# A vision block on one Trainium2 core: the attention operand stack stored as 128 rows, the position tables written in one transfer, and an earlier start

## What is computed

```
h = einsum('bhid,oi,od->bho', x, weighted_sum, weight)        # 32 x 512 x 256
q, k, v = heads of layernorm(h) @ W + b                        # 16 heads of 16
rel = log_bucket(i - j)                                        # 128 buckets, 64 either way
c2p = take(q . pos_k, rel + 64);  p2c = take(k . pos_q, -rel + 64), swapped
probs = softmax((q . k + c2p + p2c) / scale);  h += (probs . v) @ Wo + bo
h += mixture of 8 experts, 512 tokens each, of layernorm(h)
```

## Time and profile before

| | us |
|---|---|
| median of 3 runs | 5152.89 |
| the runs | 5137.70, 5157.19, 5152.89 |
| the profiled execution, its own time | 5136.03 |
| its span in the profile | 5134.3 |
| project with set-up | 0 to 981 |
| attend | 981 to about 4315 |
| output, choice, experts | from there to 5134 |

### The profile page before, as it was taken

One profiled execution on the slowest core, in us unless ns is written; L12 is line 12 of the kernel. 1 busy time (PEld: TensorE's weight loads), 2 busy tenths in 40 slices (PEclk: granted clock), 3 DMA queues, 4 the chain that ended last, 5 costly groups with the idle time before them and its releaser, 6 DMA issues. The chain is left out here.

```text
span 5134.3 us, 108898 instructions
## 1 busy us (share of the span) xinstructions
PE 4635.4 (90%) x30952; PEld 3294.1 (64%) x30952; DVE 3490.0 (68%) x9093; ACT 2706.1 (53%) x5074; POOL 1858.2 (36%) x4429
## 2 busy tenths in 40 slices
PE   6999999589999999999999999999999997894699
PEld 4666666366666666666666666666666665673556
DVE  2333333378888878888878887888888886776511
ACT  1222222266666666667666666666666664441111
POOL 1222222144444444444444444444444443330032
PEclk9999999799999999999999999999999999886599
DMA  4767676699999999999999999999999997663033
GB/s 135 229 222 233 222 236 222 198 339 354 352 337 351 350 332 346 348 334 354 348 339 348 346 346 333 346 341 332 349 350 352 349 349 231 211 216 103 2 92 81
DMA packets 663054, 1444.73 MB, mean 281 GB/s; under 512 B 47635, under 2 KB 289731, under 8 KB 662339
## 3 DMA queue, kind: packets, MB, share of 16 engines
q1 hardware_dynamic: 656326, 1429.44, 82.3%
q0 software_dynamic: 6144, 8.52, 0.9%
HBM read 722.89 MB, written 714.89 MB: 280 GB/s over the span
## 5 line engine op out<-in xcount | busy, mean ns | idle before, releaser
L1010 DVE CUSTOM_DVE_ANT_1 a_scored<-a_ps_m_s,a_bias 128x512 f32<-128x512 f32 x2048 | 1398.6, 683 | 565.4 <-PE a_ps_m_s L878 538.9
L947 ACT ACTIVATE a_probsT<-a_ps_m_t 128x512 f32<-128x512 f32 x2048 | 1226.0, 605 | 931.6 <-PE a_ps_m_t L887 930.0
L887 PE MATMUL a_ps_m_t<-a_ident,a_scored 128*128 128x128 f32 x8192 | 1261.9, 277 | 0.5 <-ACT a_probsT L947 0.5
L941 ACT ACTIVATE a_skew_in<-a_ps_m_tab 128x512 f32<-128x512 f32 x2048 | 1124.0, 613 | 192.6 <-DMA d_skew<-a_skew_in 130.8
L887 PEld LDWEIGHTS a_ps_m_t<-a_ident,a_scored 128*128 128x128 f32 x8192 | 937.1, 141 | 437.4 <-DVE a_scored L1017 358.9
L1017 DVE TENSOR_SCALAR a_scored<-a_scored,a_top_of 128x512 f32<-128x512 f32 x2048 | 1044.5, 530 | 0.0
L827 POOL TENSOR_SCALAR_AFFINE_SELECT a_bias<-a_bias 128x128 f32<-128x128 f32 (+2 forms) x2560 | 984.0, 411 | 71.8 <-POOL a_bias L827 63.1
L818 POOL COPY a_bias<-a_high 128x128 f32<-128x128 f32 (+1 forms) x1024 | 357.9, 378 | 1741.4 <-DMA a_bias<-d_skew 1740.3
L878 PE MATMUL a_ps_m_s<-a_ident,a_bias 128*128 128x128 f32 x5120 | 901.3, 273 | 0.0
L859 PE MATMUL a_ps_m_tab<-a_tabs,a_stack 96*128 96x256 bf16 (+1 forms) x4096 | 714.3, 276 | 183.7 <-ACT a_skew_in L941 111.9
L878 PEld LDWEIGHTS a_ps_m_s<-a_ident,a_bias 128*128 128x128 f32 x5120 | 682.7, 142 | 108.3 <-issue 2.1
(11 more groups left out here) (193 smaller groups left out, 3937.9 us busy)
## 6 DMA issues: line engine op xcount, KB each, us to landing
d_skew<-a_skew_in SPq DMA_DIRECT2D x1024, 480.0 KB, 7.7
a_bias<-d_skew SPq DMA_DIRECT2D x512, 896.0 KB, 8.8
a_stack<-d_stack SPq DMA_DIRECT2D x256, 384.0 KB
p_xt<-in_xT SPq DMA_DIRECT2D x32, 2048.0 KB, 9.2
d_ctx<-a_ctx_sb SPq DMA_DIRECT2D x128, 256.0 KB, 7.8
d_stack<-p_part_q SPq DMA_DIRECT2D x64, 384.0 KB, 2.8
d_stack<-p_part_k SPq DMA_DIRECT2D x64, 384.0 KB, 3.4
d_v<-p_v_sb SPq DMA_DIRECT2D x32, 544.0 KB, 3.0
```

What stands on the lines that cost most here:

```text
L887: mm = pe.transpose(m_t[:, k % 2, t * P:(t + 1) * P], scored[:, hh % SCORED, t, k * P:(k + 1) * P], ident[:])
L941: nc.scalar.activation(skew_in[:, u, w, 2 * half:2 * half + 2], m_tab[:, w], ACT.Identity).then_inc(tab_kept, 1)
L947: nc.scalar.activation(turned_at(hh // GH, hh % GH, k), m_t[:, k % 2], ACT.Exp, scale=SCALE).then_inc(turned, 1)
L1010: nc.vector.tensor_tensor_reduce(split(scored[:, hh % SCORED, t]), split(m_s[:, t % 2]), extra, 1.0, -3.0e38, ALU.add, ALU.max, top_of[:, ...
```

## The change

- `d_stack` has eight lanes instead of six: lane 7 is zeros. Lane 6 holds the nine terms' rows: in the key half the key terms, in the query half ones for the queries to which they apply (all, those of tile 2 and up, those of tile 3), and three rows of ones in the key half for the tables' constant part. `d_kterm` is gone. A new constant `extra` (128 rows, two lanes) is written into lanes 6 and 7 for every batch by two transfers of 128 rows of 4 KB; the key terms follow in six small transfers over it instead of two, once the `extra` of that batch has landed.
- `key_terms` writes four groups of 32 output rows with 128 columns each (16 matmul instructions instead of 4), so that the result is 128 x 128 and not 32 x 512.
- The stack is loaded whole: one transfer of 128 rows of 2 KB a head. No ones are set in attend.
- `scores` is one matmul of 128 rows and 512 columns for each t; `tables` use 128 rows; `tabs` is 128 rows with cleared rows where there is no operand (cleared by VectorE and GpSimd, whole).
- Table writes are one transfer over 128 partitions with all 1024 columns.
- Set-up: the products `mix` come first, `x` of batch 0 is loaded from ScalarE's queue, and the four mixing tiles of batch 0 stand between TensorE's steps of the set-up.
- Start of attend: the first stack pair is loaded before `tabs`, half of `tabs` is loaded from ScalarE's queue, and the first table writes and reads stand between the loads of stacks 3 to 6.

```diff
-        d_stack = dram("d_stack", (B, NH, HD, SLOTS, SW), BF16)
+        d_stack = dram("d_stack", (B, NH, HD, LANES, SW), BF16)
...
+            @block.scalar
+            def _(act):
+                act.dma_start(xt[:, 0], xT[0].rearrange("d (c p) s -> p (d c) s", p=P)).then_inc(x_in[0], 16)
+                act.dma_start(extra_f[:], io["extra"]).then_inc(extra_in, 16)
+                act.wait_ge(extra_in, 16)
+                nc.scalar.activation(extra[:, 0], extra_f[:], ACT.Identity).then_inc(extra_set, 1)
...
             def _(pe):
+                pe.wait_ge(t_dve, 1)
+                pe.wait_ge(x_in[0], 16)
+                mix_tile(pe, 0, 0)
                 pe.wait_ge(t_dve, 6)
...
+                mix_tile(pe, 0, 1)
                 pe.wait_ge(t_dve, 7)
...
+                mix_tile(pe, 0, 2)
                 pe.wait_ge(t_dve, 8)
...
+                mix_tile(pe, 0, 3)
                 pe.wait_ge(t_dve, 19)
...
                     n = 2 * i + u
+                    for c in range(HC):
+                        sp.dma_start(d_stack[n, c * NH // HC:(c + 1) * NH // HC].rearrange("h d j x -> (h d) j x")[:, SLOTS:],
+                                     extra[:]).then_inc(extra_out, 16)
                     if not last:
...
-                    to = d_kterm[n].rearrange("t h x -> h t x")
-                    sp.dma_start(to[:, 0:3], part_t[0:NH]).then_inc(t_out, 16)
-                    sp.dma_start(to[:, 3:], part_t[NH:]).then_inc(t_out, 16)
+                    settled(sp, extra_out, 16 * HC * (n + 1), passed)
+                    to = d_stack[n, :, :, SLOTS]
+                    for j in range(QT):
+                        for side in range(2 if j < 2 else 1):
+                            at, d = (2 * j + side) * NH, 3 * side * (j + 1)
+                            sp.dma_start(to[:, d:d + 3, S + j * P:S + (j + 1) * P], part_t[at:at + NH]
+                                         ).then_inc(t_out, 16)
...
-                    mm = pe.matmul(m_t[:], kterm_w[:, c], full_k[:, c], start=(c == 0), stop=(c == HC - 1))
+                    for j in range(QT):
+                        mm = pe.matmul(m_t[j * 2 * NH:(j + 1) * 2 * NH], kterm_w[:, c], full_k[:, c, j * P:(j + 1) * P],
+                                       start=(c == 0), stop=(c == HC - 1), skip_group_check=True)
...
-                sp.dma_start(stack[0:ST, u], d_stack[b, g * SH:(g + 1) * SH].rearrange("h d j x -> (d j) h x")
-                             ).then_inc(stack_in[u], 16)
-                sp.dma_start(stack[ST:ST + TERMS, u, :, S:], d_kterm[b, :, g * SH:(g + 1) * SH]
+                sp.dma_start(stack[:, u], d_stack[b, g * SH:(g + 1) * SH].rearrange("h d j x -> (d j) h x")
                              ).then_inc(stack_in[u], 16)
...
-                half, used = P // 2, QT * TW - P // 2
-                for p0, x0 in ((0, half), (half, 0)):
-                    sp.dma_start(bass.AP(scratch, slot * P * PITCH + p0 * (PITCH + 1) + x0,
-                                         [[PITCH + 1, half], [ROW, 2], [1, used]]),
-                                 skew_in[p0:p0 + half, u].rearrange("p w t x -> p w (t x)")[:, :, x0:x0 + used]
-                                 ).then_inc(skew_out[u], 16)
+                sp.dma_start(bass.AP(scratch, slot * P * PITCH, [[PITCH + 1, P], [ROW, 2], [1, QT * TW]]),
+                             skew_in[:, u].rearrange("p w t x -> p w (t x)")).then_inc(skew_out[u], 16)
...
-            sp.wait_ge(zeroed_p, 4)
-            for g in range(SR - 1):
+            sp.dma_start(past[:], io["past"]).then_inc(past_in, 16)
+            load_stack(0, 0)
+            load_tabs(sp, 0)
+            sp.wait_ge(tabs_clear[1], 1)
+            sp.dma_start(tabs[PLAIN_AT:PLAIN_AT + LANES * (PLAIN - 1) + 1:LANES, 1], d_plain).then_inc(const_in, 16)
+            sp.dma_start(ident[:], io["ident"]).then_inc(const_in, 16)
+            for g in range(1, SR - 1):
+                if g == 3:
+                    for m in range(2):
+                        write_tables(m, m, m)
+                    read_tables(0, 0, 0)
                 load_stack(0, g)
+                if g >= 3 and g - 1 < LEAD:
+                    write_tables(g - 1, g - 1, g - 1)
+                    if g - 2 < NEXT:
+                        read_tables(g - 2, 0, g - 2)
...
-                far = max(0, t - 1) * P
-                if far:
-                    pe.matmul(bank[:, 0:far], row[:, t * P:(t + 1) * P], row[:, S:S + far], start=True, stop=False,
-                              skip_group_check=True)
-                pe.matmul(bank[:, far:], row[0:ST + 3, t * P:(t + 1) * P], row[0:ST + 3, S + far:], start=not far,
-                          stop=False, skip_group_check=True)
+                pe.matmul(bank[:], row[:, t * P:(t + 1) * P], row[:, S:], start=True, stop=False, skip_group_check=True)
...
-            nc.vector.memset(tabs[ST:, 1], 0.0).then_inc(zeroed_p, 1)
+            nc.vector.memset(tabs[:, 0], 0.0).then_inc(tabs_clear[0], 1)
             nc.vector.memset(m_ctx[:], 0.0).then_inc(zeroed_p, 1)
-            nc.vector.memset(stack[ST:, 0], 1.0).then_inc(zeroed_p, 1)
-            nc.vector.memset(stack[ST:, 1:], 1.0).then_inc(zeroed_p, 1)
```

More of the change, by code:

```diff
@@ L166, in project, with mix_tile @@
     kterm_w = sb("kterm_w", [P, HC, 2 * NH])
-    kterm_bias = sb("kterm_bias", [2 * NH, 1])
+    kterm_bias = sb("kterm_bias", [P, 1])
     minus_half = sb("minus_half", [P, QT])
     xt = sb("xt", [P, 2, ND * HC, S])
+    extra = sb("extra", [P, LANES - SLOTS, SW], BF16)
+    extra_set, extra_zero = sem("p_extra_set"), sem("p_extra_zero")
     xT = io["xT"]
     x_in = [sem(f"p_x_in{u}") for u in range(2)]
+    h_done = sem("p_h_done")
+    m_h = ps("m_h", [P, QT, H])
+    def mix_tile(pe, u, t):
+        for k in range(ND * HC):
+            mm = pe.matmul(m_h[:, t], xt[:, u, k, t * P:(t + 1) * P], mix[:, k],
+                           start=(k == 0), stop=(k == ND * HC - 1))
+        if t % 2:
+            mm.then_inc(h_done, 1)
     with ExitStack() as tctx:
@@ L254, in step @@
                         dve.wait_ge(t_dve, done[0])
+                dve.wait_ge(t_mix, 32)
+                for d in range(ND):
+                    for c in range(HC):
+                        nc.vector.tensor_tensor(mix[:, d * HC + c], ws[:, c], wd[:, d], ALU.mult)
                 dve.wait_ge(t_in, 16 * len(loads))
@@ L402, in mixing @@
                     after(pe, h_kept, 2 * (n - 1) + t // 2 + 1 if not isinstance(n, int) or n else 0)
-                for k in range(ND * HC):
-                    mm = pe.matmul(m_h[:, t], xt[:, u, k, t * P:(t + 1) * P], mix[:, k],
-                                   start=(k == 0), stop=(k == ND * HC - 1))
-                if t % 2:
-                    mm.then_inc(h_done, 1)
+                mix_tile(pe, u, t)
             def turn(n):
@@ L458, in batch @@
                 project_v(n)
-            for t in range(QT):
-                mixing(0, 0, 0, t)
             def body(i, last):
@@ L672, in attend @@
         sem("a_" + n) for n in ("const_in", "past_in", "zeroed", "zeroed_p", "past_kept"))
+    tabs_clear = [sem(f"a_tabs_clear{w}") for w in range(2)]
     stack_in = [sem(f"a_stack_in{u}") for u in range(SR)]
@@ L700, in turned_at, with load_tabs @@
         return probsT[:, a, c]
+    def load_tabs(eng, w):
+        eng.wait_ge(tabs_clear[w], 1)
+        for j in range(SLOTS):
+            part = (SIDE_B if w == 0 else SIDE_A)[j]
+            eng.dma_start(tabs[j::LANES, w], d_tab[w, part].rearrange("(h d) x -> d h x", d=HD)
+                          ).then_inc(const_in, 16)
     def early(b, hh, lag):
@@ L1752, in shape_constants @@
                       np.broadcast_to(p[:, None].astype(np.float32), (P, B * QT))], 1)
+    extra = np.zeros((P, SW), np.float32)
+    for side, start in enumerate((0, 2 * P, 3 * P)):
+        extra[p % HD // 3 == side, start:S] = 1
+    extra[p % HD // 3 == 3, S:] = 1
     heads = np.zeros((P, OCT, HC, P), np.float32)
@@ L1756, in shape_constants @@
             heads[b * NH + (c * P + p) // HD, b, c, p] = 1
-    return {"heads": heads, "pick": pick, "ends": ends, "own": own, "ident": np.eye(P, dtype=np.float32),
+    return {"extra": extra, "heads": heads, "pick": pick, "ends": ends, "own": own, "ident": np.eye(P, dtype=np.float32),
             "past": np.stack([p[None, :] < p[:, None], p[None, :] >= p[:, None]], 1).astype(np.int32),
```

101 lines of the change are left out of this document (46 added, 55 removed).

## The result

The changed kernel takes 4988.42 us (median of 4 runs, 4984.1 to 5008.23); the kernel before, run beside it, 5150.1 (4 runs, 5137.7 to 5157.19). The ratio is **0.9696, 95% interval 0.9663 to 0.9729**: 162 us faster, where 83 were predicted, and inside the range. The profiled execution is the slowest of the four, 5008.23. The profiled execution of the kernel before, 5136.03, is the fastest of its own, so the spans differ by less than the medians do.

A forecast was written before the change was run, and what follows sets the result against it. Transfers were taken to bound attend's heads, with TensorE right behind. Terms -25 (steady heads) - 36 + 2 (project) - 9 (set-up) - 15 (start of attend) = -83 us, from 5152.9 to 5070 us; range 4970 to 5235.

The forecast's parts named there:

- What bounds attend: Attend: of 6.415 us a head about 0.26 belongs to transfers, with TensorE's floor of 6.15 us right behind.
- Steady heads: Attend's some 507 heads: from 6.415 to 6.365 us each, -25 us, between +215 and -160.
- the others: A head's transfers in attend besides the stack part: 358 GB/s before, taken as 365 after, up to 402 possible.
- whole writes: Attend's table writes: one of 1048.6 thousand bytes a head replaces two totalling 983.0; half writes at 402 GB/s taken as full speed.
- the even stack with its relief for the rest: Attend: stack load over 128 partitions goes from 245 to 380 GB/s, other transfers from 358 to 365.
- The ceiling on bytes: Rival, steady heads: memory gives only 345 GB/s, so heads cost 6.75 us, +170 us; 5265 us in all; chance 0.22.
- Stack loads were all the trouble: Rival, steady heads: other transfers reach 400 GB/s beside aligned loads, heads fall to 6.1 us, -160; 4935 us; chance 0.14.
- Scores: Attend: two matmuls and two weight loads a head go, worth 0, up to -50 us at TensorE's floor; extra rows cost nothing.
- Project: Key terms save 1.2 us a batch over 31 batches, -36 us; transfers cost 0, cover nearly gone, last batch +2 us.
- late `x`: Rival, project: x lands late, SP and the queue set the batch, the 36 us are not gained; 5105 to 5138; chance 0.14.
- Set-up: Before project: batch 0's mixing moves into the set-up block, which ends about 5.5 us later; -9 us, from -14 to -3.
- Start of attend: First scores near 1010 instead of 1036.96, without ones and with two queues; costed as -15 us, from -28 to -5.

The follow-up runs named there:

- e12: Changed kernel with the old order at the start of attend and attend's loops unrolled over eight batches instead of four: 4943.75 us, ratio 0.9622.
- e6: Changed kernel with the old order at the start of attend, seven stack loads and the values ahead of the first table write: 4977.28 us, ratio 0.9671.
- e1: Kernel before with one edit, table writes in one transfer over 128 partitions with all 1024 columns: 5090.38 us, ratio 0.9914.
- e2: Changed kernel with table writes back in two transfers of 64 partitions with 960 columns: 5028.96 us, ratio 0.9794.
- the eight profiles: Changed kernel twice and six variants, all with whole table writes, 128-partition stack loads and the loop unaltered: first to last scores 3175 to 3209 us, average 3190.
- the second profile: Changed kernel itself run and profiled again, nothing altered: 4988.3 us, ratio 0.9705; span 4977.7 us.
- e4: Changed kernel with the stack part of the scores cut into two matmuls again for t = 2 and 3: 4995.58 us, ratio 0.9717.
- e8: Changed kernel with two more 512 KB writes a batch in project, ahead of the load of x, into an unread tensor: 5014.36 us, ratio 0.975.
- e7: Changed kernel with batch 0's four mixing tiles back alone at the start of project, products and load of x staying early: 4993.1 us, ratio 0.9698.

## Why the prediction was right, and where it was short

**What bounds attend: right.** Transfers held a head up and TensorE stood right behind. After the change a head without loop turns takes 6.15 us in e12, the floor read from the earlier trace rows, and TensorE is busy 2927 of 3000 us.

**Steady heads, -25 predicted, -64 and -92 by the two profiles, -83 on average of eight: the term that was mis-sized.** The working took stack loads from 245 to 380 GB/s and "the others" from 358 to 365, and charged the whole writes for their added bytes. The rate of the stack is right: 386 alone (e6), with 240 before. What failed is the price of the **whole writes**. Their 65.6 thousand bytes at 358 GB/s stood in the sum as 65.6 / 358 = +0.18 us a head, +93 us; they bring -34 in the heads of e1 and -35 against e2's (-44 and -48 by the medians of the whole). The prediction read the half writes' 402 GB/s as full speed. But that stretch has nothing but the halves, back to back, and alone they are as fast as whole writes (404); what they cost shows only with reads beside them, whose packets take 171 ns and not 160. Why is open: back to back one half may fill what the other leaves, but no run shows which engines stood idle.

The other term, the even stack with its relief for the rest, was too large: from whole writes alone, (2000.8 + 65.6) / 358 + 0.83 = 6.60, down to 6.365, so -0.235 us a head or -119 us; from e1's 3238 us to the 3190 of the eight profiles it is -48, some -0.1 a head. No run has the new load without the rest of the change, so this is a difference of runs. The two errors, 127 us one way and some 70 the other, have opposite signs, and the forecast missed only what is left of them, some 58 us: that it lies so near is in part luck. Put as its rate, the others moved at 2066.4 / (6.28 - 0.69) = 370 GB/s, or 374, not at the 365 taken.

The Trainium skill, "SBUF — State Buffer", section "Door 1: The DMA port swizzle", says that a transfer in 64 partitions reaches half the ports and about half the bandwidth. The sign agrees with e1 and e2; the size does not: 34 or 35 us over 507 heads is 0.07 us a head, where the prediction's two figures by that rule, 4.5 and 2.4, lie 2.1 apart, and alone the halves ran at 402 GB/s. Reading the row as the end of the matter was too plain: the row holds for halves alone, and the rule's sign, though not its size, for halves among reads.

**The ceiling on bytes: refuted.** Chance 0.22 for 345 GB/s as what the memory gives. It gave 373 and 376 GB/s over 3 ms of the changed kernel, 379 in e12. The Trainium skill, "DMA: Bandwidth & Descriptors", section "Specifications", has about 358 GB/s a core as the memory's limit; over these 3 ms the traces do not agree, by 4 to 6%.

**"Stack loads were all the trouble" (4935): wrong as a cause, near in place.** The result lies between it and the forecast, and heads did fall nearly to TensorE's floor; but a third to a half of the gain in steady heads came with the writes and no stack touched (e1: 34 of 64 to 98). The sign given for it, TensorE busy 97% or more with a DMA share under 1, came by half: 2913 of 3000 us in the second profile, at a share of 1.00. The floor is reached only between loop turns, which neither had counted, and it is 6.15, not 6.1.

**Scores: right at 0** (e4). The added rows were not undone in any run; with them a head without loop turns takes 6.15 us, as long as the floor read before, so they cost nothing that shows.

**Project: right in time and in each link.** 39 us gained, 34 forecast (31 batches at 1.2 us are 37, not the 36 of the sum). 0.64 us for 16 matmuls (0.6 forecast), 1.26 us a batch (1.2), `x` in time with 0.6 us left (cover nearly gone), and the cover's end shown by e8. The rival of a late `x` did not come.

**Set-up: -9 predicted, -8.4 measured, with luck in it.** The block of set-up ends 7.8 us later; 5.5 was forecast, though the terms as written, 3 x 3 + 3 - 2.77, make 9.2. In the trace the constants land 5.9 us later (3 forecast), `mix` gives its 2.77, and what is left for the tiles in the chain is 4.7 (9 forecast). The first turn comes 8.4 us earlier; as it lies at 69.1 in e1 with the old set-up, and at 62.5 to 64.1 with the new, a gain of 5 to 10 is what is shown. e7 prices its main part, the moved mixing, at 13 us of the stage, so the rest of the new set-up costs some 4.

**Start of attend: right, for a reason only partly seen.** First scores came at 968, forecast near 1010 from an attend that began at 984, so 22 us sooner after its begin where 27 were forecast; it was costed at 15 because the transfers behind it are the limit. Just that is the 5.53 us stall at head 3. The interleaved order alone gains 8 us and loses them (e6); what is left of the gain belongs to the ones and the second queue, which were not tried apart.

Sum by stage: -8.4 set-up, -38.7 project, -21.7 start, -63.8 heads, +4.8 behind: -127.8, the difference of the two spans. By medians it is -162: the profiled execution before lies 14 us under its median and the one after 20 above. The second profile, with 28 us more in steady heads, has a sum of -156.6.

## What to carry to other kernels

When transfers limit a stage, look at each one's shape over partitions before its bytes: padding a load from 96 to 128 rows (by a difference of runs) and writing 64 columns that nobody reads (by itself, e1) were repaid, and cutting a transfer in two was free as long as each part covered all partitions. Price an uneven transfer by a run that changes the shape alone: the uneven load lost most by its own rate, the half writes by what they did to the reads beside them. And a rate read where one kind of transfer follows itself is no rate for that kind among others.

## What was not expected of the hardware

- Loads of 128 partitions by 2 KB ran at 386 GB/s alone, 96 partitions with their few key terms at 240, 96 and 32 at 248; the same bytes cut as 96 and 32 cost 160 us of 4988, cut by head nothing.
- Half and whole table writes alone ran at 402 and 404 GB/s, and yet among reads the whole ones saved 34 us in the heads.
- At each turn of a loop of 64 heads TensorE stands for some 4.5 us with no releaser in the profile.
- A DMA share of 1.00 or 1.01 goes with 345, 373 and 379 GB/s in the same stage of three kernels: it says that engines hold packets, not how fast they go.
